# A transformer block on one core: x^T of the first group moved to ScalarE's DMA queue, and four turned orders on VectorE, GpSimd and TensorE

## What is computed

```python
def ada_rms(x, t, w, tw):
    n = x * rsqrt(mean(square(x), -1, keepdims=True) + EPS)
    return n * (w * (1.0 + t @ tw.T))[:, None, :]

h = ada_rms(x, time_emb, ln1_w, ln1_tw)
q, k, v = h @ Wq.T, h @ Wk.T, h @ Wv.T          # 8 query heads, 1 key/value head
q, k = apply_rope(q, pos_ids), apply_rope(k, pos_ids)
attn = softmax(q @ k.T / sqrt(HD))               # within each sequence of 32 tokens
x = x + (attn @ v) @ Wo.T
h = ada_rms(x, time_emb, ln2_w, ln2_tw)
out = x + (silu(h @ Wg.T) * (h @ Wu.T)) @ Wd.T
```

## Time and profile before

| what | value |
|---|---|
| median of 3 runs | 111.94 us (111.45 to 113.13) |
| the profiled execution, whole time | 111.97 us |
| its span, first to last instruction | 110.1 us |
| granted TensorE clock | 1.000 of full speed |
| PE busy | 105.0 us, 95% |
| DVE, ACT, POOL busy | 66.8, 52.2, 61.5 us |

### The profile page before, as it was taken

One profiled execution on the slowest core, in us unless ns is written; L12 is line 12 of the kernel. 1 busy time (PEld: TensorE's weight loads), 2 busy tenths in 40 slices (PEclk: granted clock), 3 DMA queues, 4 the chain that ended last, 5 costly groups with the idle time before them and its releaser, 6 DMA issues.

```text
span 110.1 us, 2397 instructions
## 1 busy us (share of the span) xinstructions
PE 105.0 (95%) x772; PEld 97.2 (88%) x772; DVE 66.8 (61%) x170; ACT 52.2 (47%) x139; POOL 61.5 (56%) x92
## 2 busy tenths in 40 slices
PE   5979989999999999999999999999999999999990
PEld 4847757768999988999999999999999999999990
DVE  1476876889987945547948436479484354666311
ACT  5082768777757265214872245145623622544300
POOL 1005786399899997955489972264342420555500
DMA  3799999600000000000020000000200000200011
GB/s 69 154 374 414 313 354 421 255 9 0 0 0 3 0 0 6 0 0 9 0 95 0 0 0 6 0 3 0 95 6 0 0 0 6 98 0 0 0 48 48
DMA packets 3708, 7.66 MB, mean 70 GB/s; under 512 B 625, under 2 KB 1649, under 8 KB 3697
## 3 DMA queue, kind: packets, MB, share of 16 engines
q1 hardware_dynamic: 3552, 7.51, 19.6%
q10 hardware_dynamic: 144, 0.01, 0.1%
HBM read 6.47 MB, written 1.05 MB: 68 GB/s over the span
## 4 chain that ended last, share of the span: by engine, by line
PE 64%; POOL 16%; DMA 6%; DVE 5%; issue 4%; SPq 2%; ACT 0%; DVEq 0%; POOLq 0%; ACTq 0%
PE ps_gu L410 31%; DMA xt<-in_xT 6%; POOL hf_l L1078 3%; POOL wgu_l L1086 3%; PE ps_d L263 3%; PE ps_a L264 3%; PE ps_a L265 3%; PE ps_d L265 3%; PE ps_a L263 3%; PE ps_d L264 3%; PE ps_a L363 3%; PE ps_s L375 2%; POOL wd_l L1092 2%; PE ps_gu L319 2%; DVE rot_b L609 2%
## 5 line engine op out<-in xcount | busy, mean ns | idle before, releaser
L1078 POOL TENSOR_TENSOR hf_l<-hf,hf_h 128x256 fp32r<-128x256 f32 x32 | 23.8, 742 | 25.6 <-ACT hf_h L958 25.6
L410 PE MATMUL ps_gu<-h_h,wgu_h 128*128 128x256 f32 x120 | 25.2, 291 | 0.0
L951 ACT ACTIVATE th<-ps_gu 128x256 f32<-128x256 f32 x32 | 12.3, 383 | 25.2 <-PE ps_gu L410 24.5
L410 PE MATMUL ps_gu<-h_h,wgu_l 128*128 128x256 f32 x120 | 23.9, 280 | 0.0
L410 PE MATMUL ps_gu<-h_l,wgu_h 128*128 128x256 f32 x120 | 23.9, 280 | 0.0
L742 DVE SCALAR_TENSOR_TENSOR sg<-th,ps_gu 128x256 f32<-128x256 f32 x32 | 13.3, 415 | 16.1 <-ACT th L951 16.0
L410 PEld LDWEIGHTS ps_gu<-h_h,wgu_h 128*128 128x128 f32 x120 | 18.6, 189 | 0.2
L410 PEld LDWEIGHTS ps_gu<-h_l,wgu_h 128*128 128x128 f32 x120 | 18.4, 188 | 0.0
L410 PEld LDWEIGHTS ps_gu<-h_h,wgu_l 128*128 128x128 f32 x120 | 18.3, 188 | 0.0
L958 ACT ACTIVATE hf_h<-hf 128x256 fp32r<-128x256 f32 x32 | 13.2, 411 | 8.7 <-DVE hf L751 8.6
L751 DVE TENSOR_TENSOR hf<-sg,ps_gu 128x256 f32<-128x256 f32 x32 | 13.4, 420 | 1.0
(11 more groups left out here) (136 smaller groups left out, 200.4 us busy)
## 6 DMA issues: line engine op xcount, KB each, us to landing
wgu<-in_w_gu SPq DMA_DIRECT2D x4, 512.0 KB, 9.3
xt<-in_xT SPq DMA_DIRECT2D x4, 256.0 KB, 6.9
wd<-in_w_d SPq DMA_DIRECT2D x2, 512.0 KB, 12.5
out_x<-xk SPq DMA_DIRECT2D x3, 256.0 KB, 2.1
pb<-in_pack_b SPq DMA_DIRECT2D x1, 576.0 KB, 6.6
xk<-in_x_tok SPq DMA_DIRECT2D x2, 256.0 KB, 8.1
xk<-in_x_tok SPq DMA_DIRECT2D x1, 512.0 KB, 11.4
wqkv<-in_w_qkv SPq DMA_DIRECT2D x1, 320.0 KB, 5.7
```

Source lines behind the costliest of these rows:

```text
L410: mm = pe.matmul(ps_gu[:, slot % RING, part, cols], w[:, m, span(part * KH + k, 1, P)], h[:, k, cols], start=(step == 0 and k == 0), stop= ...
L951: act.activation(th[:, n % RING], ps_gu[:, n % RING, 0, :], ACT.Tanh, scale=0.5).then_inc(th_ready, 1)
L1078: pool.tensor_tensor(hf_l[:, m], hf[:, m], hf_h[:, m].bitcast(F32), ALU.subtract).then_inc(hf_lo, 1)
```

## The change

The load of `xt[0]` goes from the third place of SP's queue to the first of ACT's, ahead of `small`. SP's later loads move up one place. On PE, `qkv(2, 1, 1)` goes ahead of `scores(0, 1, 1)`. On DVE, `low_x2(0, 1)` goes ahead of `add_rotation(1, 0)`. On POOL, during the MLP of group 0, `low_down(1)` and `root_2(1)` go earlier and both `late_rotate_b` go later. No operation is added or taken away. Since SP's block is one line shorter, the lines between L189 and L872 have numbers one lower in the changed kernel.

```diff
         def _(sp):
             sp.dma_start(pa[:, :], pack_a).then_inc(in_pa, 16)
             sp.dma_start(pos_sb[:, :], pos).then_inc(in_pos, 16)
-            sp.dma_start(xt[:, 0], xT[:, 0]).then_inc(in_xt[0], 16)
             sp.dma_start(wqkv[:, :, :], w_qkv).then_inc(in_wqkv, 16)
...
             turn_mod()
+            qkv(2, 1, 1)
             scores(0, 1, 1)
-            qkv(2, 1, 1)
             turn_probs(0, 0, 1)
...
             rotate_a(1, 0)
+            low_x2(0, 1)
             add_rotation(1, 0)
-            low_x2(0, 1)
             turn_qk(1, 0, 1)
...
         def _(act):
+            act.dma_start(xt[:, 0], xT[:, 0]).then_inc(in_xt[0], 16)
             act.dma_start(small[:, :], pack_s).then_inc(in_small, 16)
...
             low_hidden(0, 2)
+            low_down(1)
+            low_hidden(0, 3)
+            low_hidden(0, 4)
             late_rotate_b(2, 0)
-            low_hidden(0, 3)
+            root_2(1)
+            low_hidden(0, 5)
+            low_hidden(0, 6)
             late_rotate_b(2, 1)
-            low_hidden(0, 4)
-            low_down(1)
-            low_hidden(0, 5)
-            root_2(1)
-            low_hidden(0, 6)
             low_hidden(0, 7)
             late_rotate_a(2)
```

## The result

The changed kernel is slower: 115.29 us median of 4 runs (113.96 to 116.17) against 112.19 for the kernel before (111.45 to 113.13, 4 runs). The ratio is 1.020, 95% interval 1.0146 to 1.0254. The interval lies above 1, but on both sides of the 2% that the forecast took as the least change that can be told. The profiled execution took 114.42 us, its span is 112.2 against 110.1. So the profile has to explain 2.1 us of span, and the two late times something on top.

A forecast was written before the change was run, and what follows sets the result against it. PE bounds the MLPs of groups 1 to 3, so the time is PE's entry there plus a constant. +0.45 + 0.2 - 0.17 - 0.65 = -0.17 us on 111.97 gave 111.8, called no change; range 111.0 to 113.0.

The forecast's parts named there:

- The delay of the angles: DVE's start of the angles, waiting for small behind xt[0] on ACT's queue: 0.45 us later than 4.15.
- the high end of 1.8: Upper bound on the angles' delay: small lands together with xt[0] at 5.9 us, 1.8 us late.
- both small loads took 3.0 to 3.2 us with or without a big load ahead: Loads of pos and small at the start: the reason for taking the angles' delay nearer its low end, at 0.45 us.
- The first rival: Slower: at the start xt[0] and pa share engines, pos and small come behind; delay 0.93 to 1.8, time 112.5; chance 0.28.
- Without slack, so d goes onto PE in full: From the angles to the first q/k/v products: the angles' delay, taken as 0.45 us, reaches PE undiminished.
- the gain of 0.2 that I counted for SP's earlier loads: x^T of group 2 lands earlier, bringing kbd of tile 1 forward by 0.2 us, but not PE.
- The turned product on PE: qkv(2, 1, 1) ahead of scores(0, 1, 1) in the prologue: pushes the scores later, taken as +0.2 us.
- low_x2 early: DVE's low part of h2 sooner: PE's 0.32 us wait before 25.43 goes, taken as -0.17 us; ends 0 and -0.32.
- 0.1 for the semaphore: Hand-over from POOL's kbd of group 1 (row ends 28.59) to PE's scores: 0.1 us, leaving about 0.17 to gain.
- POOL's order: End of group 0's MLP: PE's waits at 41.12 and 43.74 go, 0.69 us; taken as -0.65, ends -0.1 and -0.7.
- of 0.45 after the semaphore, plus about 0.15 that POOL gains: Slack between kbd of group 2 (ends 49.39) and PE's scores (49.93), said to let 0.6 to 0.69 us pass.
- the third rival: POOL's gains return as a wait for kbd of group 2 or the root: -0.1 for -0.65, 112.35 us; chance 0.1.

The follow-up runs named there:

- e2: Kernel before with only the load of xt[0] moved to the front of ACT's queue, all orders as before; ratio 1.0178.
- e4: Kernel before with pos ahead of pa on SP's queue and xt[0] on ACT's queue behind small and the first activation; ratio 1.0200.
- e3: Changed kernel with small issued ahead of xt[0] on ACT's queue; ratio 1.0040, median 114.01 us of ten runs.
- e10: Kernel before with half of xt[0] (128 KB) ahead of small on ACT's queue, the other half in its old place; ratio 1.0028.
- e1: Changed kernel with the load of xt[0] back in its old place on SP's queue, the four turned orders kept; ratio 1.0018, median 111.99 us.
- e5: Kernel before with the change's new order on POOL alone; ratio 1.0045.
- e6: Kernel before with another order on POOL alone: low_down(1) early, but both late_rotate_b ahead of root_2(1); ratio 0.9979.
- e7: Changed kernel with two blank matmul calls more before the first product and two more before the mean squares; 113.87, 113.98, 114.19, 115.78 us.
- e8: Kernel before with other queues: small, pos, xt[0] on ACT's; pa, wqkv and the rest on SP's; ratio 1.0291.
- e12: Changed kernel with PE's order in the prologue put back as before; ratio 1.0151.
- e9: Changed kernel with two blank matmul calls more before the first product and eight more before the mean squares; 114.89, 115.04, 115.09, 115.31 us.
- e11: Kernel before with low_x2(0, 1) early, both late_rotate_b ahead of root_2(1) on POOL, four narrow blank matmuls more on PE; ratio 0.9938, median 111.40 us.

## Why the prediction was wrong

- **The delay of the angles: failed, and it alone decides the sign.** The step is "I take d = 0.45". Measured: 2.24 in the changed kernel, 2.6 in e2, outside even the high end of 1.8. It took 0.25 us for what the 256 KB ahead of small cost beyond its later issue. The rate for it was that of the window at 6 to 7 us (392 GB/s); from 2 to 5 us it was 199 to 252 in after, and two big loads issued together each took 5.0 to 5.6 us (after, e2, e4). And the argument "both small loads took 3.0 to 3.2 us with or without a big load ahead" read as a fixed cost what was the cost of pa: pos stood behind it and small went out beside it, and in e4, with neither, they took 1.7 and 1.9. The first rival named the place and the direction; I had given it 0.28, and a price of at most 1.8. By the Trainium skill (page "DMA: Bandwidth & Descriptors", section "Issuing engines are not separate DMA queues") loads started by different engines run on the same 16 DMA engines and interleave. The trace of after agrees: pa took 5.0 instead of 3.0. That pa kept its 3.0 in e3, where the other big load was issued 0.43 us later, the rule does not tell.
- **"Without slack, so d goes onto PE in full": failed, by 0.47.** From the angles to kbd of tile 1 it is 9.47 us in after and 9.94 before. It looks like the gain of 0.2 that I counted for SP's earlier loads, but e10 has the same 9.47 with x^T of group 2 issued where it was. It is slack: before, POOL was held up by that load and not by the angles, as the prediction's own first paragraph says, so 0.47 of the delay cost nothing. With the angles 2.24 late, a load that lands earlier gives nothing.
- **The turned product on PE: right sign, +0.34 for +0.2.** Counting what waits for the scores, not PE's own work, was the right way to read it. In e1, with the loads in their old places, it is +0.04.
- **low_x2 early: the wait went, the gain of -0.17 did not come.** The wait before 27.25 is gone and one of 0.26 us for kbd is there; the scores of group 1 come 4.76 us after the first MLP product, 4.77 before. The step that failed is "0.1 for the semaphore": from the end of kbd's row to the scores it is 0.25 to 0.27 us in every trace in which PE waited for it (0.26 in after), and it was already 0.27 before (28.59 to 28.86). There was no slack.
- **POOL's order: the waits went as forecast, the gain did not stay.** The step that failed is the slack "of 0.45 after the semaphore, plus about 0.15 that POOL gains". With 0.26 for the hand-over instead of 0.1 the slack was 0.28. And POOL gained nothing: an idle time of 0.52 us before `low_hidden(0, 7)` was gone, but it idled 0.41 us for the sums of squares, and two `low_hidden` took 1.88 us in place of 1.43, while DVE computed `low_down(3)` beside them. kbd of group 2 came 0.23 us later behind the first MLP product (24.92 against 24.69), which leaves 0.28 - 0.23 = 0.05 us of gain. That is the third rival (-0.1 for -0.65), given 0.1; e5 shows it alone and e6 undoes it. For those 1.88 us the overlap is what the trace shows; the cause was not tried.
- **The sum.** With the right d the sum of the working is 2.24 + 0.2 - 0.17 - 0.65 = 1.6. With the measured terms, in the same order the delay, the slack, PE's product and both other orders together: 2.24 - 0.47 + 0.34 + 0 = 2.11, which is the span's difference.
- **What was not in the working at all** is the clock. It was named only as what would make everything wrong. The traces show it in two forms. In e3, e6, e7 and e8 PE had been idle for 2.0 to 2.6 us ahead of the mean squares, and the granted clock was then 0.50 for about 3 us. In e2 and e12 that idle time was 0.8 and 1.3 us and the granted clock reads 1.00, yet the weight loads took 0.34 us until about 13 us. From the first q/k/v product to the first MLP product e2 and e6 lost about 1.3 us against e10, and e7 1.5 against after. The changed kernel's two late executions have no trace; their mean clocks were 1.000 (116.16) and 0.982 (116.17), so there may be one of each form. The delay at the start is not needed for this: of 58 executions of the kernel before that were timed beside e1 to e12, 13 had a mean clock of 0.982 to 0.985, and their times were 113.3 to 114.8. A later start does leave PE idle longer ahead of the mean squares (0.6 us before, 2.1 after), and e9 has neither that idle time nor late times. With four executions of each kernel that speaks for the idle time, but doesn't show it.

## What to carry to other kernels

A second DMA queue added no rate here (199 and 226 GB/s from 2 to 4 us with a big load on each, 228 and 210 before). What goes out beside or ahead of the loads that are needed first can delay them, so order the loads over both queues by when they are needed, and don't put a few KB that start a chain behind a few hundred. Ask of a delay, too, what else holds up the place where it arrives: 0.47 of 2.24 us were free here. When a queue's order is changed to remove a wait, look for the next semaphore that the engine behind it feeds, and fill the engine's own new idle time with the work that was pushed back. And look at what a delay at the start leaves idle: in four traces TensorE came back from 2.0 to 2.6 us of idle time at half its clock, though not in the changed kernel's own.

## What was not expected of the hardware

- Where pa (288 KB) and xt[0] (256 KB) went out together, pa took 4.5 to 5.5 us and xt[0] 4.9 to 5.6 (after, e2, e4, e7, e9, e12); with no second load of 256 KB or more issued at the same moment pa took 2.8 to 3.1 (before, e1, e3, e5, e6, e8, e11), and 3.3 beside one of 128 KB (e10). Issued 0.43 us apart (e3), with pa first, pa was not slowed at all. Why so little makes so much difference stays open.
- ACT issues a DMA that stands behind an activation in its program before that activation has run: in e4 the load went out at 1.2 us, and the activation ahead of it ran at 2.46, behind a table load of 1.28 us:

```profile
1.23 0.39 ACTq L970 DMA_DIRECT2D xt<-in_xT  x1
2.46 0.20 ACT L969 ACTIVATE primed<-blank 128x1 f32<-128x1 f32 x1
```

- In the first 6 us PE's matmuls ran at half rate in several traces (`pa`'s weight loads 0.33 us each in before, 0.19 in after), with a granted clock of 1.00 in the windows. In e2 and e12 this went on until about 13 us. The column does not show this state; the duration of a weight load does.
- The granted clock fell behind an idle time of 2.0 to 2.1 us in e6 and e7 and not in the profiled execution of after. What decides between them stays open.
